# Cross-attention kernel: the normalised context turned by VectorE in 32 by 32 blocks instead of by TensorE

## The reference

```
for layer in (1, 2):
    h = layer_norm(x);  q = h @ wq + bq                    # 16 heads of 128
    k, v = ctx @ wk + bk, ctx @ wv + bv, and one extra key/value row (bias_k, bias_v)
    p = softmax(q k^T / sqrt(128))                          # over 1501 keys
    x = x + (p v) @ wo + bo
x = x + gelu(layer_norm(x) @ w_fc1 + b_fc1) @ w_fc2 + b_fc2
```

## Time and profile before

| | us |
|---|---|
| median of 3 runs | 1302.52 (1300.93 to 1304.53) |
| the profiled execution, its own time | 1303.02 |
| its span (first to last instruction) | 1301.2 |
| PE busy in it | 1245.8 (96%) |
| POOL busy | 902.6 (69%) |
| ACT busy | 806.5 (62%) |
| DVE busy | 795.3 (61%) |
| mean granted TensorE clock | 0.984 of 2.4 GHz |

### The profile page before, as it was taken

How to read it: one execution, slowest core, us unless ns; L and a number is a source line. 1 busy time by engine, 2 the same in 40 slices (tenths; PEclk the granted TensorE clock), 3 DMA queues, 4 the chain that set the end, 5 groups by cost and what they waited for, 6 DMA issues and landing times.

```text
span 1301.2 us, 27136 instructions
## 1 busy us (share of the span) xinstructions
PE 1245.8 (96%) x8016; PEld 1144.4 (88%) x8016; DVE 795.3 (61%) x1368; ACT 806.5 (62%) x1572; POOL 902.6 (69%) x750
## 2 busy tenths in 40 slices
PE   6999999999999999989699999999999999999887
PEld 5779999999999998978686999999999999999787
DVE  6855666666666666537684666666656666664554
ACT  4745666666666666666384666666666666667554
POOL 4737777777777686667572768686868786867772
PEclk9999999999999999999899999999999999999898
DMA  5401111111111111122251111111111111101231
GB/s 174 130 9 48 37 60 37 57 43 59 49 50 47 47 47 35 36 59 64 80 165 36 37 36 60 35 59 38 56 45 61 36 59 35 59 24 45 57 90 31
DMA packets 30426, 72.69 MB, mean 56 GB/s; under 512 B 3072, under 2 KB 4144, under 8 KB 30368
## 3 DMA queue, kind: packets, MB, share of 16 engines
q1 hardware_dynamic: 30368, 72.01, 18.0%
HBM read 71.52 MB, written 0.48 MB: 55 GB/s over the span
## 4 chain that ended last, share of the span: by engine, by line
PE 85%; DVE 5%; ACT 3%; issue 3%; DMA 1%; POOL 1%; DVEq 0%; ACTq 0%; POOLq 0%; SPq 0%
PE psum L621 34%; PE psum L642 13%; PE psum L644 12%; PE psum L643 12%; PE psum L591 5%; PE psum L675 4%; PE psum L653 2%; DVE g_prod L1091 1%; PE psum L628 1%; PE psum L635 1%; PE psum L612 1%; ACT slots L925 1%; DMA w_raw<-weights 1%; DVE t_max L1154 1%; PE psum L666 1%
## 5 line engine op out<-in xcount | busy, mean ns | idle before, releaser
L486 POOL TENSOR_TENSOR pt<-slots,pt 125x512 fp32r<-125x512 f32 (+1 forms) x384 | 444.6, 1162 | 217.7 <-ACT slots L894 185.3
L621 PE MATMUL psum<-qs,ctx 128*125 128x384 f32 (+1 forms) x2304 | 540.9, 371 | 4.7 <-DVE qs L1131 2.4
L621 PEld LDWEIGHTS psum<-qs,ctx 128*125 128x125 f32 x2304 | 394.4, 186 | 50.6 <-ACT slots L925 9.5
L642 PE MATMUL psum<-ctx,pt 125*128 125x258 f32 x1344 | 385.8, 287 | 5.2 <-ACT on L900 4.2
L643 PE MATMUL psum<-ctx,pt 125*128 125x256 f32 x1344 | 379.3, 282 | 0.0
L644 PE MATMUL psum<-ctx,pt 125*128 125x258 f32 x1344 | 379.2, 282 | 0.0
L1154 DVE TENSOR_TENSOR t_max<-psum,t_max 125x512 f32<-125x512 f32 (+1 forms) x320 | 199.5, 623 | 261.8 <-PE psum L621 261.2
L893 ACT ACTIVATE pt<-slots 125x512 fp32r<-125x512 f32 (+1 forms) x384 | 221.7, 577 | 191.7 <-DVE slots L1142 178.3
L925 ACT ACTIVATE slots<-psum 125x512 f32<-125x512 f32 (+1 forms) x384 | 207.5, 541 | 145.4 <-DVE t_max L1154 135.0
L642 PEld LDWEIGHTS psum<-ctx,pt 125*128 125x128 f32 x1344 | 253.6, 189 | 22.8 <-ACT on L900 14.7
L643 PEld LDWEIGHTS psum<-ctx,pt 125*128 125x128 f32 x1344 | 254.1, 189 | 6.0
(11 more groups left out here) (84 smaller groups left out, 1045.5 us busy)
## 6 DMA issues: line engine op xcount, KB each, us to landing
nat_stage<-ctx_nat SPq DMA_DIRECT2D x64, 375.0 KB
tr_stage<-ctx_tr SPq DMA_DIRECT2D x64, 375.0 KB, 3.1
w_raw<-weights SPq DMA_DIRECT2D x72, 256.0 KB, 2.7
dk_all<-dk_rows SPq DMA_DIRECT2D x2, 768.0 KB, 6.5
dk_all<-dk_rows SPq DMA_DIRECT2D x2, 256.0 KB, 3.8
xres<-x_rows SPq DMA_DIRECT2D x4, 112.0 KB, 2.2
out_rows<-xres SPq DMA_DIRECT2D x4, 112.0 KB, 2.0
bo<-out_bias SPq DMA_DIRECT2D x1, 336.0 KB, 3.8
```

The lines of the kernel that those rows point to most:

```text
L486: nc.gpsimd.tensor_tensor(split_weights(h, LO, c), slot(h, c), as_f32(split_weights(h, HI, c)), ALU.subtract).then_inc(pt_lo, 1)
L621: last = mm(scores(h, k), ctx_tr_chunk(half, a, c), qs[h][:, m, half, 0:R], start=(half, a, m) == terms[0], stop=(half, a, m) == terms[-1])
L642: mm(O_BANK[j][:, 0:D + 2], hi, ctx_nat_hi(c), start=(c == 0), stop=False, skip_group_check=True)
```

## The change

All groups but a layer's last are now turned by DVE. Its transpose works on blocks of 32 by 32. One instruction takes the 32 query rows and every fourth block of 32 dims: it reads 32 partitions of `on` and writes 32 partitions of a new tile `turn`, 4 x 2 x 32 = 256 elements each for group 0 and 192 for group 1. A group needs 16 of them. The table `TURNS` tells in which step how many stand. ACT then copies the whole of `turn` to `qt` at once, for group 0 in step 16 (128x1024) and for group 1 in step 23 (128x768). The last group of a layer goes through PE as before. DVE waits with normalising a group until the group before has been turned. To make room for `turn`, `bo` holds one bias row at a time, loaded anew by SP for each of the three sums.

```diff
+TURNS = {6: 2, 7: 2, 8: 2, 10: 2, 11: 2, 12: 2, 14: 2, 15: 2, 18: 3, 19: 3, 20: 4, 21: 2, 22: 4}
+QUARTER, QUARTERS = 32, 4
+BLOCKS = QUARTERS * QUARTERS
-        bo = sb("bo", [RGP, 3, D], F32)
+        bo = sb("bo", [RGP, D], F32)
+        turn = sb("turn", [P, DC, GT[0] * P], F32)
...
+            def load_bias(m):
+                sp.wait_ge(xb_ready, INIT + m * RG)
...
                             pe.wait_ge(max_done, INIT + group * (NCT - 1))
-                            pe.wait_ge(ot_out, INIT + group * 2 - 4)
+                            pe.wait_ge(max_ready, INIT + group - 1)
                             max_transposes(1 - h)
...
-                        if c in (6, 8) and not first:
-                            if c == 6:
-                                pe.wait_ge(max_ready, INIT + group)
-                            group_transposes(b - 1, h, c // 2 - 3, OT_BANK)
...
                 def normalized(b, h):
                     act.wait_ge(rden_ready, INIT + l * GROUPS + b * 2 + (h + 1))
+                    act.wait_ge(turned, INIT + l * TURNED + b * (2 * BLOCKS) + h * BLOCKS)
...
+                def turned_context(b, h):
+                    act.wait_ge(turned, INIT + l * TURNED + b * (2 * BLOCKS) + (h + 1) * BLOCKS)
+                    go(qt_flat[:, :, ds(b * FLAT + h * GT[0] * P, GT[h] * P)], turn[:, :, 0:GT[h] * P],
+                       ACT.Copy).then_inc(turn_out, 1)
...
-                        if c in (6, 8) and not first and not (tail and h == 1):
-                            transposed_context(b - 1, h, c // 2 - 3)
+                        if k in (NCT + 4, STEPS - 1) and not first:
+                            turned_context(b - 1, 1 if k == STEPS - 1 else 0)
...
+                def turn_context(b, h, i):
+                    if i == 0:
+                        dve.wait_ge(on_act, INIT + l * (2 * GROUPS) + b * 4 + (2 * h + 2))
+                        dve.wait_ge(on_dve, INIT + l * (3 * B) + b * 3 + (2 + h))
+                        dve.wait_ge(turn_out, INIT + l * (GROUPS - 1) + b * 2 + h)
+                    rows, dims = i // QUARTERS * QUARTER, i % QUARTERS * QUARTER
+                    source = on[rows:rows + QUARTER, 0:GT[h]].rearrange(
+                        "r j (c q d) -> r j c q d", c=DC, q=QUARTERS)[:, :, :, i % QUARTERS]
+                    goal = turn[dims:dims + QUARTER, :, 0:GT[h] * P].rearrange(
+                        "d c (j q r) -> d j c q r", j=GT[h], q=QUARTERS)[:, :, :, i // QUARTERS]
+                    V.transpose(goal, source).then_inc(turned, 1)
...
+                        if k in TURNS and not first:
+                            done = sum(n for at, n in TURNS.items() if at < k)
+                            for i in range(done, done + TURNS[k]):
+                                turn_context(b - 1, i // BLOCKS, i % BLOCKS)
```

More of the change, by code:

```diff
@@ L231, in build @@
         ot_mm, ot_out = sem("ot_mm"), sem("ot_out")
+        turned, turn_out = sem("turned"), sem("turn_out")
         pn_picked = sem("pn_picked")
@@ L238, in build @@
         settled = sem("settled")
-        N_TABLES, N_CONSTS = 2, 4
+        N_TABLES, N_CONSTS = 2, 3
         def settle(eng):
@@ L248, in build @@
             "pe": [w_used, xt_mm, q_mm, qp_mm, lb_mm, lb_spread, s_mm, mt_mm, nb_mm, pv_mm, ot_mm, pn_picked, c_mm, y_mm],
-            "act": [w_hi, h_hi, q_hi, qp_out, first_qs_hi, copied, exp_done, pe_done, on_act, ot_out,
+            "act": [w_hi, h_hi, q_hi, qp_out, first_qs_hi, copied, exp_done, pe_done, on_act, ot_out, turn_out,
                     p80_hi, oth_hi, c_hi, g32_ready],
@@ L252, in build @@
                     dv_ready, gp_ready, gp_used, q_lo, first_qs_lo, lb_rows_ready, nat_hi, tr_hi, lb_ready, max_done,
-                    mt_reduced, max_ready, px_ready, sub_done, den_ready, rden_ready, pn_ready, on_dve, p80_lo,
+                    mt_reduced, max_ready, px_ready, sub_done, den_ready, rden_ready, pn_ready, on_dve, turned, p80_lo,
                     oth_lo, c_lo, xb_ready],
@@ L333, in load_weight @@
                 sp.dma_start(w_raw[u][:], weights[ds(job, 1)].rearrange("a p n -> (a p) n")).then_inc(w_in[u], 16)
+            def load_bias(m):
+                sp.wait_ge(xb_ready, INIT + m * RG)
+                settle(sp)
+                sp.dma_start(bo[:], out_bias[ds(m, 1), :].rearrange("a n -> (a n)").partition_broadcast(RGP)).then_inc(
+                    bo_in, 16)
             def load_nat(batch, n, p):
@@ L397, in batch_loads @@
                             load_tr(b + 1, tr + p, p)
+                load_bias(l)
                 batch_loads(0, True, False)
@@ L410, in _ @@
                         load_weight(l * JOBS + quad * 4 + (H + 4 + u), u, None)
+            load_bias(LAYERS)
             for u in range(4):
@@ L763, in group_contexts @@
                     last.then_inc(pv_mm, 1)
[L765 to L773, removed]
                 def batch_steps(b, first, tail):
@@ L813, in _ @@
                 last.then_inc(pn_picked, 1)
-                group_transposes(B - 1, 1, 0, OT_BANK)
-                group_transposes(B - 1, 1, 1, OT_BANK)
+                pe.wait_ge(on_act, INIT + (l + 1) * (2 * GROUPS))
+                pe.wait_ge(on_dve, INIT + (l + 1) * (3 * B))
+                context_transposes(0, 2, OT_BANK)
+                pe.wait_ge(ot_out, INIT + l * 2 + 1)
+                context_transposes(2, GT[1], OT_BANK)
                 heads, jobs = l * H, l * JOBS + H
@@ L945, in _ @@
                     weight_hi(l * JOBS + (H + u), u, l * 8 + 4)
-                transposed_context(B - 1, 1, 0)
-                transposed_context(B - 1, 1, 1)
-                act.wait_ge(ot_out, INIT + (l + 1) * (2 * GROUPS))
+                last_context(0)
+                last_context(1)
+                act.wait_ge(ot_out, INIT + (l + 1) * 2)
+                act.wait_ge(turn_out, INIT + (l + 1) * (GROUPS - 1))
                 def context_hi(h, s, free):
@@ L1038, in add_bias @@
             def add_bias(m):
+                dve.wait_ge(bo_in, m * 16 + 16)
+                settle(dve)
                 for g in range(RG):
-                    V.tensor_tensor(xres[:, g, :], xres[:, g, :], bo[:, ds(m, 1), :].rearrange(
-                        "p a d -> p (a d)"), ALU.add).then_inc(xb_ready, 1)
+                    V.tensor_tensor(xres[:, g, :], xres[:, g, :], bo[:], ALU.add).then_inc(xb_ready, 1)
             def nat_part_hi(n, p):
@@ L1181, in normalized @@
                     dve.wait_ge(rden_ready, INIT + group + 1)
-                    dve.wait_ge(ot_mm, INIT + group * 2)
+                    dve.wait_ge(turned, INIT + l * TURNED + b * (2 * BLOCKS) + h * BLOCKS)
                     for j in range(1, n, 2):
```

12 lines of the change are left out of this document (6 added, 6 removed).

## The result

The change makes the kernel slower: **1326.99 us** median (1325.59 to 1329.46) against 1303.53 of the kernel before on the same chip, a ratio of **1.0184** with a 95% interval of 1.0168 to 1.0200. The prediction, 1291 us in a range of 1284 to 1311, missed by 36 us, and with the wrong sign.

A forecast was written before the change was run, and what follows sets the result against it. PE was taken to bound the kernel, busy 63.21 of a batch's 63.40 us. The terms -23.3 + 1.0 + 4.9 + 5.6 = -11.8 us gave 1291 us against the median, 0.9% faster, in a range of 1284 to 1311.

The forecast's parts named there:

- the late maximum: Steps 18 to 23: DVE's turns delay maximum 23, holding PE's transposes of the maxima 0.4 us a batch, +5.6 us.
- ACT's copy: Step 16: the copy ahead of step 17's normalisation, for which PE waits, costs 0.35 us a batch, +4.9 us.
- the turns of steps 6 to 15: Twelve turns in steps 6 to 12 and four in 14 and 15, 7.2 us on DVE, have room and cost nothing.
- PE's saving: Transposes taken off PE save 1.54 us in a batch, 23.3 us over both layers; 1.0 given back in the tail.
- The price of a turn: On DVE, a turn takes 0.45 us for 256 elements and 0.38 for 192, without overlap.
- The first and third rivals: DVE turns at 0.33 and 0.26 us, about 1285 us, chance 0.18; or 0.456 us, a draw near 1301, chance 0.16.
- the walk: Steps 18 to 23: DVE's start times added up instruction by instruction at 0.38 us a turn, maximum 23 at 364.02.
- The slack ahead of the DMA: Behind maximum 21 the cast of `nat_stage` waits for its DMA until 358.19, which swallows up to 0.52 us of lateness.
- The fourth rival: Steps 18 to 23: DVE becomes the bound through late maximum 23; slower, about 1311 us at 0.50 us a turn; chance 0.27.
- What was to show it: Signs: batch near 62.6 us, DVE busy up 181 us, PE waiting near 0.4 us for `t_max`, ACT's step-17 idle gone.

The follow-up runs named there:

- the steady cast: The changed kernel with DVE's cast of `tr_stage` written as a reduction over an axis of length 1: 1310.34 us, ratio 1.0064.

## Why the prediction was wrong

The forecast's batch was 63.40 - 1.54 + 0.35 + 0.40 = 62.61 us; it took 65.21, so 2.60 more. Over the seven distances of a layer the forecast is 441.9 - 7 x 0.79 = 436.4 us and 453.1 was measured: 33.5 us over both layers, of the 36 us of the miss. Three terms of the sum failed: the late maximum (0.40 forecast, 1.71 measured), ACT's copy (0.35 and 0.88), and the turns of steps 6 to 15, put at nothing, which cost 0.58 in step 13.

- **PE's saving: right.** 23.3 less 1.0 was forecast. Without turns and with the copy out of the way the batch is 1.64 shorter (1.54 forecast), the ratio of 0.9819 is 23.6 us (20 to 27).
- **The price of a turn: right, within 0.02.** 0.45 and 0.38 from start to start were forecast; with 436 and 369 ns and a gap of 0.03 it is 0.46 and 0.40. The first and third rivals are ruled out by their condition.
- **ACT's copy, 0.35 a batch: mis-sized, 0.88.** The step that failed is that I took the start of ACT's score copy, 344.73, from the kernel before as it stood. The four turns of steps 14 and 15 made ACT 0.63 later, in the same batch whose turns I "cost at nothing". Alone the copy costs 0.26, with the turns 0.88: priced one by one, both looked harmless.
- **Turns in steps 6 to 15 at nothing: wrong.** I asked whether the maximum is late for the scores of two steps later, but not who waits for the subtraction. Two waiters were missed: ACT's exponentials, above, and in step 13 PE's spreading of the maxima, 0.58 us a batch, 8 us. With the turns of step 12 moved to step 13 that wait was gone. The two turns of step 12 stand between `p_extra` and that subtraction. There `p_extra` itself grew from 0.37 to 0.82 us, and ended 0.03 behind the instruction that POOL was running (343.17 and 343.14).
- **The late maximum, 0.40 a batch: mis-sized, 1.71.** This is the largest term: 1.31 us too little in each of 12 batches is 16 us (the last batch of a layer has little of it), and the steady cast gave 16.7 us back. The table holds the walk against DVE's rows of the kernel after, less 7.60 us (PE takes up step 17 at 353.92 instead of 346.32).

| start of | walk | measured | late by |
|---|---|---|---|
| first turn of step 18 | 350.63 | 351.27 | 0.64 |
| maximum 19 | 352.37 | 353.06 | 0.69 |
| maximum 20 | 354.59 | 355.45 | 0.86 |
| maximum 21 | 357.19 | 358.24 | 1.05 |
| cast of `nat_stage` | 358.19 | 358.70 | 0.51 |
| maximum 22 | 360.42 | 361.09 | 0.67 |
| maximum 23 | 364.02 | 365.25 | 1.23 |
| PE's transposes of the maxima | 364.61 | 365.93 | 1.32 |

Rows of DVE in the kernel after from which it comes:

```profile
358.87 1.16 DVE L1211 STREAM_TRANSPOSE turn<-on 32x192 f32<-32x192 f32 x3
...
360.66 0.55 DVE L1166 TENSOR_TENSOR t_max<-psum,t_max 125x384 f32<-125x384 f32 x1
361.25 1.17 DVE L1211 STREAM_TRANSPOSE turn<-on 32x192 f32<-32x192 f32 x3
...
366.30 0.94 DVE L1060 CAST ctx<-nat_stage 125x768 fp32r<-125x768 f32 x1
...
370.63 1.58 DVE L1211 STREAM_TRANSPOSE turn<-on 32x192 f32<-32x192 f32 x4
...
372.85 0.55 DVE L1166 TENSOR_TENSOR t_max<-psum,t_max 125x384 f32<-125x384 f32 x1
```

The cast of step 18 gives 0.64: it takes 1.59 to the next start (357.28 to 358.87) where the walk had 0.69, less 0.26 by which it began earlier. That of step 22 gives 0.48 (369.15 to 370.63 is 1.48, the walk had 1.0). Between them the turns give 0.41, partly because the first turn behind a maximum starts 0.59 behind the maximum's start and not 0.48: it does not overlap with it. The slack ahead of the DMA did swallow 0.54, as the walk said. So the logic of the walk held, and the input that failed by much is the length of a cast, taken from the schedule of before. I had the spread of 543 to 1708 ns in the earlier trace rows and used it as an argument about turns, not about the cast itself. The trace of the kernel before already held the pattern. There the cast of step 18 ends 0.40 us behind POOL's instruction too (350.70 and 350.30):

```profile
349.94 0.76 DVE L1054 CAST ctx<-tr_stage 128x750 fp32r<-128x750 f32 x1
...
349.00 1.30 POOL L486 TENSOR_TENSOR pt<-slots,pt 125x512 fp32r<-125x512 f32 x1 [1.98 <-DVE ctx L1048]
```

- **The fourth rival, half right.** Its outcome and its place came true: slower, by the late maximum 23. Its condition did not: it asked for a turn above 0.464 us, and the turn takes 0.40. It should have been written as "DVE's other instructions get longer when they are shifted", with the 1708 ns row as its price.
- **What was to show it.** PE's transposes gone and DVE's busy time up: yes (by 215 us, not 181: the turns' 194, and 15 of the other 21 the casts of `tr_stage`). The wait on the maximum near 0.4 us: no, 1.24 to 1.28 in twelve batches and 0.26 in the last of each layer. ACT's idle time ahead of normalising gone: yes.

## What to carry to other kernels

Work that is moved to an engine with 24 us of free time in 63 is paid for at its deadlines, not in its busy share: before pricing a moved instruction, list every engine that waits for what is queued behind it, and price the added instructions together, in one walk over all engines. Where an instruction's duration varies threefold in the trace of before, find out beside what it is long and where the change will shift it; its old length is no input for the new schedule. And compare periods of a repeated stage between traces: here they told 0.26 us a batch, which the medians of whole executions could not.

## What the runs showed of the hardware that was not expected

- **A cast on DVE that waits for POOL's instruction.** In the kernel after POOL was busy when each of the 64 casts of `tr_stage` began. 62 of them end 0.40 to 0.41 us behind the end of that POOL instruction, the other two 0.44 and 0.45; in the kernel before it is 0.40 to 0.41 in 63 of 64. Over all kernels such a cast is 541 to 1875 ns long; written as a reduction over an axis of length 1 it takes 914 to 935 ns, whatever POOL does. Tiny DVE operations with both inputs in SBUF stretch likewise: `pn_extra`, 128 by 4 elements or fewer, takes 150 to 156 ns in the kernel after where POOL is idle at its start (16 times), and 351 to 839 where it is not (16 times), ending 0.02 us behind POOL's instruction.
- **A stall costs more than its listed idle.** Where PE ran through before, 1.25 us listed cost 1.71, and 0.32 cost 0.58. The idle time is counted from the end of the last matmul, while a successor without a wait starts before that end (363.47 with 1.56 us, the next at 364.87). Where there was a wait already, at step 17, the difference of the listed values (0.86) is the cost (0.88). So the three listed totals of the kernel after, 32.5 us more than before, stand for about 44 us: the 22.4 us that the batches are longer, and the 1.54 x 14 = 21.6 us that PE saves in them.
- **A transpose on DVE rarely overlaps with its neighbours.** 32x256 in float32 takes 436 ns and 32x192 369. Of the 480 turns, 450 start 0.03 us behind the end of the instruction ahead of them, where other pairs overlap by 0.08. The 30 others, each the first turn of a group, start 0.08 before that end (357.28 + 1.67 against 358.87 above). The prediction weighed a rule of the Trainium skill ("VectorE: DVE Perf Modes", "Two Vector instructions with no wait between them"): an instruction is held if its input or output starts in another 32-partition quarter than the last one's. The trace agrees in all 480 turns. The first turn of a group starts in the first quarter on both sides, as the instruction ahead of it does, so the prediction's "every turn here changes its output quarter" is wrong for those 30.
